# Products of zeros on TensorE between the products of a causal attention

## What is computed

```python
hd = 128 // 16
q = (layer_norm(x) @ q_w + q_b) / math.sqrt(hd)
k = layer_norm(x) @ k_w + k_b
v = layer_norm(x) @ v_w + v_b
scores = einsum('bhqd,bhkd->bhqk', split(q), split(k))
scores = where(tril(ones((s, s))), scores, neg)       # s = 1024
attn = softmax(scores, axis=-1)
ctx = einsum('bhqk,bhkd->bhqd', attn, split(v))
```

## Time and profile before

| | us |
|---|---|
| median of 3 executions | 3865.84 |
| lowest, highest | 3863.87, 3868.72 |
| the profiled execution, its own time | 3869.13 |
| its span, from the first to the last instruction | 3867.4 |
| TensorE busy (share of the span) | 3359.5 (87%) |
| VectorE busy | 2608.5 (67%) |
| GpSimd busy | 1648.3 (43%) |
| ScalarE busy | 1513.0 (39%) |
| mean granted clock of TensorE, as a share of 2.4 GHz | 0.905 |

### The profile page before, as it was taken

How to read it: one execution, slowest core, us unless ns; L and a number is a source line. 1 busy time by engine, 2 the same in 40 slices (tenths; PEclk the granted TensorE clock), 3 DMA queues, 4 the chain that set the end, 5 groups by cost and what they waited for, 6 DMA issues and landing times. The chain is left out here.

```text
span 3867.4 us, 51915 instructions
## 1 busy us (share of the span) xinstructions
PE 3359.5 (87%) x18323; PEld 1886.7 (49%) x18323; DVE 2608.5 (67%) x4185; ACT 1513.0 (39%) x1843; POOL 1648.3 (43%) x1064
## 2 busy tenths in 40 slices
PE   3896969668434699999999999999999999999977
PEld 2554636333231255555555555555555555554535
DVE  6787868755307877777777777778778778773221
ACT  4332313224220044444444444444444444444432
POOL 1222212210130046555555555555556556566650
PEclk8897969756665589999999999999999999999988
DMA  1000000000040000000000000000000000000000
GB/s 56 0 0 0 0 0 0 0 12 1 22 120 6 0 1 1 1 3 2 1 3 2 1 3 2 1 3 2 1 3 2 1 3 1 2 1 1 1 24 6
DMA packets 20389, 27.87 MB, mean 7 GB/s; under 512 B 5064, under 2 KB 12368, under 8 KB 20048
## 3 DMA queue, kind: packets, MB, share of 16 engines
q1 hardware_dynamic: 18832, 21.83, 1.8%
q0 software_dynamic: 1344, 3.15, 0.3%
HBM read 21.30 MB, written 3.67 MB: 6 GB/s over the span
## 5 line engine op out<-in xcount | busy, mean ns | idle before, releaser
L2082 POOL TENSOR_TENSOR pair_total_pool<-pair_total_pool,pair_probs 128x1024 f32<-128x1024 f32 (+2 forms) x456 | 1334.3, 2926 | 918.9 <-DVE pair_total L2046 880.4
L1969 ACT ACTIVATE pair_probs<-banks 128x1024 f32<-128x1024 f32 (+1 forms) x944 | 961.8, 1026 | 1138.0 <-PE banks L1863 1127.0
L1999 DVE TENSOR_REDUCE pair_peaks<-banks 128x1 f32<-128x512 f32 (+1 forms) x1680 | 1094.9, 672 | 239.4 <-PE banks L1844 199.0
L1887 PE MATMUL banks<-pair_probs,pair_values 128*64 128x512 f32 (+1 forms) x3776 | 863.1, 598 | 0.0
L1844 PE MATMUL banks<-pair_k_high,pair_q_high 64*128 64x512 f32 (+1 forms) x1920 | 707.4, 465 | 66.9 <-DVE pair_peaks L1992 50.0
L2046 DVE TENSOR_TENSOR pair_total<-pair_total,pair_probs 128x512 f32<-128x512 f32 x464 | 445.5, 960 | 207.1 <-POOL pair_total_pool L2082 155.0
L1844 PEld LDWEIGHTS banks<-pair_k_high,pair_q_high 64*128 64x128 f32 x1920 | 307.3, 196 | 441.2 <-issue 354.5
L1863 PE MATMUL banks<-pair_q_shift,pair_one_rows 64*128 64x512 f32 (+1 forms) x1888 | 512.4, 432 | 6.1 <-ACT pair_probs L1969 5.9
L1863 PE MATMUL banks<-pair_q_high,pair_k_high 64*128 64x512 f32 (+1 forms) x1888 | 494.4, 392 | 0.0
L1863 PE MATMUL banks<-pair_q_high,pair_k_low 64*128 64x512 f32 (+1 forms) x1888 | 493.4, 391 | 0.0
L1887 PEld LDWEIGHTS banks<-pair_probs,pair_values 128*64 128x64 f32 (+1 forms) x3776 | 249.4, 136 | 463.4 <-issue 400.5
(11 more groups left out here) (306 smaller groups left out, 3295.6 us busy)
## 6 DMA issues: line engine op xcount, KB each, us to landing
expert_w<-in_fc SPq DMA_DIRECT2D x32, 256.0 KB, 3.7
context_rows<-in_ctx SPq DMA_DIRECT2D x10, 320.0 KB, 5.2
dense_w<-in_We SPq DMA_DIRECT2D x2, 1024.0 KB
experts_in<-expert_zeros SPq DMA_DIRECT2D x1, 1024.0 KB, 3.8
expert_b<-in_fc_b SPq DMA_DIRECT2D x2, 512.0 KB, 4.7
expert_rows<-experts_in SPq DMA_DIRECT2D x16, 64.0 KB, 1.9
experts_out<-expert_result POOLq DMA_DIRECT2D x4, 256.0 KB, 4.5
row_parameters<-in_rows SPq DMA_DIRECT2D x1, 896.0 KB, 7.4
```

The source lines that it names most:

```text
L1887: last = pe.matmul(out[heads[head], c, :], values[0:n, (g * BLOCKS + i // 4) % 2, i % 4, heads[head]], probs_of(i)[0:n, c, head, :], start ...
L1969: act.activation(probs_of(i)[0:n, c], slot(e)[0:n], ACT.Exp, scale=1.0 / 8.0).then_inc(S["expd"].sem, 1)
L1999: v.reduce_max(peaks[:, head, t, b:b + 1], fill_banks(f)[:, head, 0:width(b)], axis=AX).then_inc(S["peaked"].sem, 1)
L2082: pool.tensor_tensor(pooled[0:rows_, first:3], pooled[0:rows_, first:3], probs_of(i)[0:rows_].rearrange("p c h n -> p (c h) n")[:, first + ...
```

## The change

Behind `causal_parts` a tile `causal_nothing` of 128 by 384 in type fp32r is made and, in a block of its own, cleared by VectorE. In TensorE's program one product is put in front of every fill, score and accumulation for which the output banks are open, that is from behind accumulation 0 to ahead of accumulation 7 of each group. It multiplies 128 rows by 128 columns of zeros with 128 rows by 256 columns of zeros and adds the result to half of bank 7, where the output of the group accumulates. It stands ahead of the wait for a pair of banks and waits for nothing itself. No other engine's instructions change but for VectorE's clear.

```diff
@@ causal_attention
+        nothing = k.sb("causal_nothing", [P, P + 256], F32R, ctx=ctx)
         causal_parts(k, xaT, spare, context, queries_by_row, keys_by_row, values, zeros, mask, peaks, sent)
...
+        cleared = k.sig("causal_nothing_cleared")
+        with nc.Block() as block:
+            @block.vector
+            def _(v):
+                v.memset(nothing[:].bitcast(F32), 0.0).then_inc(cleared.sem, 1)
+                v.wait_ge(cleared.sem, 1)
+
         with nc.Block() as block:
             @block.tensor
             def _(pe):
...
+                def add_nothing():
+                    pe.matmul(out[:, 1, 0:256], nothing[:, 0:P], nothing[:, P:P + 256], start=False, stop=False)
+
+                opened = False
                 for unit in order:
                     kind, g = unit[:2]
                     if kind == "keep":
                         continue
+                    if opened and unit[0] in ("add", "fill", "score"):
+                        add_nothing()
                     if kind == "add":
                         add(*unit[1:])
+                        opened = unit[2] < TT - 1
                         continue
                     if place[unit] >= SLOTS:
                         wait_taken(pe, units[place[unit] - SLOTS])
```

## The result

| us | before | with the change |
|---|---|---|
| median of 4 executions | 3864.86 | 3927.31 |
| lowest, highest | 3861.84, 3868.72 | 3924.42, 3930.96 |
| span of the profiled execution | 3867.4 | 3923.8 |
| the four stretches, accumulation 0 to 7, together | 124.7 | 181.9 |
| TensorE busy | 3359.5 | 3436.1 |

The ratio is 1.0162, with a 95% interval of 1.0144 to 1.0179. The kernel became 62 us slower. The prediction said 8 us faster, with a range that ends at 3875 us: it was wrong in sign and in size.

What follows compares the result with a forecast made beforehand. TensorE, often at its low clock, was taken to bound the causal attention. Products +9.2, clock -18.5 and block +0.9 gave -8.4 us: median 3857.4 us, range 3847 to 3875 us.

Steps and rivals of the forecast that it cites:

- 0.33 us for each of the 28 pieces between two accumulations: +9.2 us: Causal attention on TensorE: exposed cost of the zero products at the high clock, 2 x 0.115 plus 0.10 us a piece.
- a product on all rows also parts the 25-row products: Middle of each piece: full-array products separate 25-row products that run side by side; 0.10 us a piece added.
- The bound that it named: Upper bound on the zero products' cost in the causal attention: all 142 paid at the low clock, 30.5 us.
- The products of zeros that stand before that wait mostly run in it: Between two accumulations: products ahead of the last fill's 0.66 us wait for ScalarE are mostly hidden in that wait.
- What the clock gives back: Four causal stretches, accumulation 1 to 7: higher TensorE clock shortens pieces by 20.5 us, nine tenths taken, -18.5 us.
- being busy isn't enough here: TensorE before clock changes: busy throughout both times, clock rose only behind full-array transposes, not behind products on part of the array.
- The block in front: Extra block before the attention: VectorE clear 0.35 us plus block edge 0.5 us, everyone waits, +0.9 us.
- Rival 1: Causal stretches: zero products don't move the clock, all 142 paid at 1.2 GHz; +21 us, 3887 us; chance 0.15.
- Rival 2: Causal pieces: lost overlap of 25-row products costs another 0.3 us in each of 28, 3866 us; chance 0.17.
- Rival 3: Causal stretches: clock rises but doesn't hold, only half of the 20.5 us comes, 3866 us; chance 0.13.
- The checks: New profile's causal pieces: first 0.3 us longer, accumulation 1 to 3 some 9.5 us, 3 to 6 some 8.5 us.
- The bound for being wrong: Four causal stretches, 124.7 us before: forecast is wrong if together they don't fall below 118 us.

## Why the prediction was wrong

The prediction's sum was 9.2 - 18.5 + 0.9.

- **"0.33 us for each of the 28 pieces between two accumulations: +9.2 us"** is the step that failed: the four stretches grew by 57.2 us, 2.0 us for each piece. Its price of a product came from neighbours of the same shape, which start 0.43 and 0.23 us apart; these follow products of their own shape. Between units of 25 rows a product costs its columns and two changes of shape, beside an accumulation its columns and one, and all that stood side by side is strung out. Measured at the same clock: 0.60 us each at 0.50 and 0.18 us each at 1.00, over whole pieces, waits included. The prediction added 0.10 us a piece for "a product on all rows also parts the 25-row products"; the piece of four units shown above grew by 5.02 - 2.21 = 2.81 us. The bound that it named, all 142 at the low clock for 30.5 us, was no upper bound at all, since it holds columns alone. The Trainium skill (TensorEngine Tiling (Array Packing), Tiling Modes, Key Properties) says it in words: "Mode switching requires drain", where a mode is a height of 32, 64 or 128 rows together with a width of 32, 64 or 128 columns. The trace agrees: 1.13 us for a product and a unit with 64 as with 128 rows, no cost to be seen with 32, and 0.51 us from a product to an accumulation of another width. The prediction did not weigh that rule.
- **"The products of zeros that stand before that wait mostly run in it"** The earlier trace rows would have held if the products had the assumed price. The wait of 0.59 us in that piece is gone, but 2.81 us more than fill it. Over the four stretches TensorE's idle time fell from 24.8 to 4.7 us, so some 20 us were hidden, and 57 us were not. (The prediction also misread a row here: at 969.67 us ScalarE starts its work on the score, it doesn't end it. Nothing in the sum hangs on that.)
- **"What the clock gives back", -18.5 us,** did not come: the stretches have 0.60, 0.63, 0.56 and 0.90 instead of 0.85 and more. Groups 0 and 1 rose by 0.05 and 0.04, group 3 by 0.12, and group 2 fell by 0.26. The reason is not that zeros count for nothing: in a row they gave 0.96, 0.71, 0.95 and 0.94, and 64 of them gave 0.96, 0.81, 0.81 and 0.90. Spread out they left TensorE busy for 20.44 of 20.44 us at 0.50 throughout; with two products at each place groups 1 and 2 had 0.86. That the changes of shape took the clock with them is argued from these rows and not shown by a run. The prediction's own sentence, "being busy isn't enough here", was right, and it was not applied to a TensorE that is busy with changes of shape.
- **"The block in front", +0.9 us,** was right: 1.0 us by the timeline, and 1.8 us between medians, with an interval of the ratio that holds 1.
- **The rivals.** Rival 1 was right on slower, and both of its marks are in the profile, a clock near 0.6 and stretches over 40 us, but for another reason; its 3887 us are 40 us short. Rival 2, the lost overlap, came nearest to the mechanism, with its price of 0.3 us for a piece too low by a factor of nine in the piece read (2.81 us); it had no cost for the change of shape itself. VectorE's waits for fills grew, as it said: in group 0's stretch from 14.7 to 26.8 us, by the rows below. Its other sign, a high clock, is missing. Rival 3's sign, a clock that changes every few us, is there in group 0; its time of 3866 us is not.

VectorE's waits in group 0's stretch (releaser, us in total, times, longest), before and then with the change:

```profile
DVE causal_piece_peaks L991 <- PE banks L931: 14.7, 10, 3.8
```

```profile
DVE causal_piece_peaks L1006 <- PE banks L939: 26.8, 14, 4.3
```

- **The checks.** The first piece of each group was to grow by 0.3 us; group 0's went from 7.26 us (846.97 to 854.23) to 10.54 us (848.23 to 858.77). Accumulation 1 to 3 was to take 9.5 us and took 874.87 - 858.77 = 16.10 us in group 0; 3 to 6 was to take 8.5 us and took 20.44, 17.34 and 20.19 us in the long groups.
- **The bound for being wrong**, stretches that don't fall below 118 us, was met by 182 us. With 64 products in a row they did fall below, to 115.5 us.

Does the price of a change account for the time? An estimate: in group 3's piece 9 products bring 12 more changes of shape, 12 x 0.2 + 9 x 0.115 = 3.4 us, less the 1.9 us that TensorE was idle there before: 1.5 us, and 1.65 us were measured. Counting changes of height alone (6 of the 12) it would be 0.3 us. In group 0's piece 15 products bring 24 changes, 24 x 0.3 + 15 x 0.215 = 10.4 us, less 0.85 us of idle time: 9.6 us, and 8.97 us were measured. The estimate leaves out the lost overlap of fills and scores.

What stays open. How the 57 us divide between the changes of shape and the clock that did not rise: at the low clock 0.60 us a product, at the high clock 0.18 us; were all 142 like those of group 3's piece they would cost 142 x 0.18 = 26 us, so about half of the loss may hang on the low clock; that is an estimate, since that piece has scores alone and much idle time to hide in, and no run held the clock and kept the changes. Whether products with other numbers than zero lift the clock more was not tried. Nor were products of 32 rows on all four parts of the array at once. Which places for rows of products raise the clock most is open too: 64 behind two accumulations gained, 78 behind all of them did not, in one execution. And the low clock's place in group 0 changes from one execution to the next (0.55 and 0.71 with the same instructions); no run shows why.

## What to carry to other kernels

Price an instruction set between others by neighbours of another shape, not of its own: on TensorE a change between products of another height or width cost some 0.2 us at the high clock and 0.3 us at the low one, and it undid the overlap of everything around it. Filler for the clock belongs in a row, or has the shape of the work around it: 64 in rows behind two accumulations of each group gained 5 us, and 142 spread out lost 62 us. Before calling a sum of columns an upper bound, ask what else the instruction does to the ones beside it.

## What the hardware showed that was not expected

- A change of shape costs the same from 25 rows to 64 and to 128 rows (1.13 us for a product and a unit in both), the same again from 128 columns to 32 at equal height (0.51 us from the product's start in both cases), and nothing to be seen to 32 rows.
- Twice the products were no slower: the four stretches took 175.1 us with 284 and 181.9 us with 142. The second of two costs 0.11 us at the high clock, and the clock is 0.86 in place of 0.63 in group 1. Each has one profiled execution.
- TensorE busy without any gap stayed at 1.2 GHz for 20.44 us, while with 25.59 of 32.78 us busy it had 0.96 (142 products in rows).
- Products whose operands are all zeros do lift the clock: 0.911 to 0.915 over whole executions with 142 in rows, 0.904 to 0.908 without.
